# Fused two-layer block on one core: eight expert steps over the undispatched tiles stand behind the dispatched row tiles, with gates, result slots and routing drawn elsewhere

## The reference, cut to what matters

```python
logits = normed @ router_w.T
probs = softmax(logits)
top_v, top_i = top_k(probs, 2)
gates = softmax(top_v)
comb = sum(one_hot(top_i, E) * gates[..., None], axis=1)
for e in range(E):
    out = out + comb[:, e, None] * swiglu(normed, gate_up_w[e], down_w[e])
out = out + swiglu(normed, shared_gate_up_w, shared_down_w)
x = x + tanh(g_ffn[1]) * out
```

## Time and profile before

| what | value |
|---|---|
| median of 3 runs | 319.88 us (319.79 to 321.32) |
| the profiled execution | 319.61 us |
| its span in the trace | 317.8 us |
| TensorE matmul, busy | 268.3 us (84%) |
| VectorE, busy | 236.4 us (74%) |
| ScalarE, busy | 204.4 us (64%) |
| GpSimd, busy | 158.9 us (50%) |
| mean granted clock of TensorE | 0.941 |

### The profile page before, as it was taken

How to read it: one execution, slowest core, us unless ns; L and a number is a source line. 1 busy time by engine, 2 the same in 40 slices (tenths; PEclk the granted TensorE clock), 3 DMA queues, 4 the chain that set the end, 5 groups by cost and what they waited for, 6 DMA issues and landing times.

```text
span 317.8 us, 7526 instructions
## 1 busy us (share of the span) xinstructions
PE 268.3 (84%) x2406; PEld 201.9 (64%) x2406; DVE 236.4 (74%) x711; ACT 204.4 (64%) x469; POOL 158.9 (50%) x206
## 2 busy tenths in 40 slices
PE   7878986997999797999988853878899999999950
PEld 4553442555677464676766732368799999999940
DVE  3586198857977666788999967998576767677796
ACT  2964799796577588976855543535657575756560
POOL 2624297024622546643024777770047878787531
PEclk9999999899999999999999655879999999999995
DMA  7890003001269999970000011113122223111064
GB/s 211 233 383 10 1 2 132 0 3 19 117 188 185 178 181 180 190 105 0 2 1 24 30 45 40 53 49 88 37 71 68 78 67 87 51 32 33 8 226 132
DMA packets 34612, 28.12 MB, mean 88 GB/s; under 512 B 3072, under 2 KB 32389, under 8 KB 33936
## 3 DMA queue, kind: packets, MB, share of 16 engines
q1 hardware_dynamic: 32192, 23.77, 33.8%
q0 software_dynamic: 2240, 3.72, 3.6%
q10 hardware_dynamic: 144, 0.15, 0.2%
HBM read 14.15 MB, written 14.40 MB: 90 GB/s over the span
## 4 chain that ended last, share of the span: by engine, by line
PE 52%; DVE 30%; ACT 8%; issue 6%; DMA 2%; SPq 1%; POOL 1%; DVEq 0%
PE bank L1195 47%; DVE region_k L912 2%; DVE region_x L1152 2%; DVE top L911 2%; DMA wr<-in 2%; PE bank L1492 1%; DVE bn_raw L870 1%; DVE nm L1001 1%; DVE region_k L1003 1%; DVE x L1141 1%; DVE x L1142 1%; ACT x_hat L540 1%; DVE x L902 1%; PE bank L1419 1%; DVE region_k L969 1%
## 5 line engine op out<-in xcount | busy, mean ns | idle before, releaser
L1177 DVE TENSOR_TENSOR region_k<-region_x,region_k 128x768 f16<-128x768 f32 (+1 forms) x33 | 30.6, 926 | 21.6 <-ACT region_k L714 21.6
L1195 PE MATMUL bank<-w_high,region_k 128*128 (+1 forms) x380 | 37.8, 221 | 6.4 <-DVE x L1171 3.3
L1195 PE MATMUL bank<-w_scaled,w_high 128*128 128x256 f16 x252 | 42.5, 273 | 0.1
L846 POOL DMA_INDIRECT expert_rows<-region_k,slot_dest x22 | 27.1, 1232 | 26.5 <-DVE region_k L1164 19.2
L714 ACT ACTIVATE region_k<-region_x 128x768 f16<-128x768 f32 (+1 forms) x33 | 26.8, 813 | 15.8 <-DVE region_x L1152 13.7
L820 POOL DMA_INDIRECT dispatched_rows<-region_t,slot x28 | 28.8, 1028 | 16.1 <-issue 8.3
L1195 PEld LDWEIGHTS bank<-w_high,region_k 128*128 128x128 f16 x380 | 30.9, 99 | 7.7 <-issue 7.3
L1195 PE MATMUL bank<-w_scaled,w_low 128*128 128x256 f16 x126 | 34.3, 273 | 0.0
L1195 PE MATMUL bank<-w_low,region_k 128*128 (+1 forms) x190 | 34.0, 221 | 0.0
L1152 DVE SCALAR_TENSOR_TENSOR region_x<-bank,region_w 128x768 f32<-128x768 f32 (+1 forms) x33 | 30.4, 920 | 3.2 <-ACT region_w L719 2.2
L1195 PE MATMUL bank<-filler 128*128 128x512 f16 x94 | 26.9, 407 | 3.9 <-DVE region_k L912 2.4
(11 more groups left out here) (242 smaller groups left out, 736.1 us busy)
## 6 DMA issues: line engine op xcount, KB each, us to landing
dispatched_rows<-pad_rows SPq DMA_DIRECT2D x8, 1048.0 KB, 18.8
w_scaled<-in SPq DMA_DIRECT2D x5, 1024.0 KB, 8.0
w_scaled<-dispatched_rows SPq DMA_DIRECT2D x21, 131.0 KB, 2.3
region_q<-expert_rows SPq DMA_DIRECT2D x3, 512.0 KB, 5.0
x<-in SPq DMA_DIRECT2D x4, 256.0 KB, 4.4
region_w<-in SPq DMA_DIRECT2D x2, 512.0 KB, 7.0
out<-x SPq DMA_DIRECT2D x3, 256.0 KB, 2.3
w_scaled<-in SPq DMA_DIRECT2D x1, 704.0 KB, 4.1
```

The lines of the kernel that those rows point to most:

```text
L846: pool.indirect_dma_start(ytok, bass.IndirectOffsetOnAxis(dst[:, n, h:h + 1].bitcast(U32), 0), yv[n % 4][:, h * D:(h + 1) * D], None, boun ...
L1177: dve.tensor_tensor(hsplit[:, v, k:2 * k], hid[:, v, 0:k], hsplit[:, v, 0:k], ALU.subtract).then_inc(hidden_low, 1)
L1195: return pe.matmul(o, l, r, start=start, stop=stop)
```

## The change

- **Steps.** DENSE_FIRST goes from 3 to 0: 4 shared, 21 row tiles, 8 dense steps. There are 33 steps as before.
- **Routing.** For G0 and G1 the turn, logits, route, rank and slots get due times of their own, earlier than before. The sends are split into send0 to send3, one tile each, with new due times.
- **Result slots.** `slot_dest(n)` moves from row step n - 2 to row step n, behind the low part.
- **Bookkeeping.** top2_apart goes to the step of row tile 2, gates_of_all to that of tile 6, ScalarE's tanh to that of tile 4.
- **Gates and sums.** G1 goes from VectorE to ScalarE and GpSimd. ScalarE weights G2 inside the two steps 30 and 31, then G1 and G3. GpSimd adds in the order G2, G1, G3. VectorE sums G0 alone. SyncE loads results in the order G2, G0, G1, G3 and stores G2, G0, G1, G3, G4.

```diff
-DENSE_FIRST = 3
+DENSE_FIRST = 0
...
-C_POOL = {"rstd": -4.6, "early_low": -5.3, "low": -0.9, "rstd2": 6.5, "send": 12.5, "send2": 16.1}
+C_POOL = {"rstd": -4.6, "early_low": -5.3, "low": -0.9, "rstd2": 6.5, "send0": 11.3, "send1": 11.32, "send2": 11.34, "send3": 11.36}
...
-C_PE_AT = {("turn", 11): 19.95, ("logits", 11): 20.6, ("turn", 13): 21.2, ("logits", 13): 21.4, ("rank", 11): 21.5,
+C_PE_AT = {("turn", 3): 11.4, ("logits", 3): 12.4, ("rank", 3): 13.4, ("turn", 7): 15.4, ("logits", 7): 16.4, ("rank", 7): 17.4,
...
-C_ACT_AT = {("turn_out", 11): 20.55, ("norm2", 13): 20.7, ("high", 13): 20.9, ("turn_out", 13): 21.6,
+C_ACT_AT = {("turn_out", 3): 11.9, ("turn_out", 7): 15.9, ("turn_out", 11): 20.55, ("norm2", 13): 20.7, ("high", 13): 20.9, ("turn_out", 13): 21.6,
...
-C_DVE_AT = {("affine", 13): 20.8, ("low", 13): 21.0, ("route", 11): 21.4, ("slots", 11): 21.6,
+C_DVE_AT = {("low", 3): 11.25, ("route", 3): 12.8, ("slots", 3): 13.5, ("low", 7): 15.25, ("route", 7): 16.8, ("slots", 7): 17.5,
...
-C_POOL_AT = {("rstd2", 13): 19.4, ("rstd2", 15): 21.5, ("send2", 7): 21.6, ("send", 11): 21.7, ("send2", 11): 21.8, ("send", 13): 21.9}
+C_POOL_AT = {("send0", 3): 13.45, ("send1", 3): 13.6, ("send2", 3): 13.7, ("send3", 3): 13.8, ("send0", 7): 17.6, ("send1", 7): 17.7,
+             ("rstd2", 13): 18.5, ("send2", 7): 18.6, ("send3", 7): 18.7, ("rstd2", 15): 21.3,
+             **{(f"send{k}", t): t + 10.5 + 0.1 * k for t in (11, 13) for k in range(4)}}
...
-            for g in (0, 2, 1, 3):
+            for g in (2, 0, 1, 3):
                 n = slice(*GROUPS[g])
                 eng.dma_start(yk[:, n, :], ytok_v[:, n, :]).then_inc(x_loaded[g], 16)
-            for g, ready, count in ((2, last_added, 2), (0, sum_done, T), (SPARSE, rows_ready, len(STEPS)), (3, last_added, 4),
-                                    (1, sum_done, 2 * T)):
+            for g, ready, count in ((2, last_added, 2), (0, sum_done, T), (1, last_added, 4), (3, last_added, 6),
+                                    (SPARSE, rows_ready, len(STEPS))):
...
+            def gated_rows(g, c):
+
+                act.wait_ge(gates_done, 1)
+                act.wait_ge(x_loaded[g], 32)
+                for t in range(*GROUPS[g]):
+                    last = act.activation(yk[:, t, c * D:(c + 1) * D], yk[:, t, c * D:(c + 1) * D], ACT.Copy,
+                                          scale=gate[:, t, c:c + 1])
+                last.then_inc(last_gated, 1)
...
-                if s == 0:
+                if s == len(STEPS) - 3:
+                    gated_rows(2, 0)
+                elif s == len(STEPS) - 2:
+                    gated_rows(2, 1)
+                if s == STEP_OF[4]:
...
-            for g in (2, 3):
-                act.wait_ge(x_loaded[g], 32)
+            for g in (1, 3):
                 for c in range(2):
-                    for t in range(*GROUPS[g]):
-                        last = act.activation(yk[:, t, c * D:(c + 1) * D], yk[:, t, c * D:(c + 1) * D], ACT.Copy,
-                                              scale=gate[:, t, c:c + 1])
-                    last.then_inc(last_gated, 1)
+                    gated_rows(g, c)
...
+                elif stage[:4] == "send" and g is not None and g < SPARSE and lo + int(stage[4]) < hi:
+                    if stage == "send0":
+                        pool.wait_ge(padded, 16 * (E + 2))
+                        pool.wait_ge(slots_ready, g + 1)
+                        pool.wait_ge(ffn_high, g + 1)
+                        pool.wait_ge(ffn_low, g + 1)
+                    send_rows(lo + int(stage[4]))
...
-            for k, (g, c) in enumerate(((2, 0), (2, 1), (3, 0), (3, 1))):
+            for k, (g, c) in enumerate((g, c) for g in (2, 1, 3) for c in range(2)):
...
-            after_hidden = {0: top2_apart, 1: tiles_placed, 2: windows_packed, 3: gates_of_all}
+            after_hidden = {1: tiles_placed, 2: windows_packed, STEP_OF[2]: top2_apart, STEP_OF[6]: gates_of_all}
...
-                ahead = STEPS[s + 2] if s + 2 < len(STEPS) else ("", 0)
-                if ahead[0] == "rows" and ahead[1] >= 2:
-                    slot_dest(ahead[1])
...
-                if ahead[0] == "rows" and ahead[1] < 2:
-                    slot_dest(ahead[1])
+                if s < len(STEPS) and STEPS[s][0] == "rows":
+                    slot_dest(STEPS[s][1])
                 if s == len(STEPS) - 1:
                     dve.wait_ge(x_loaded[0], 32)
                     sum_rows(range(0, 1))
                 elif s == len(STEPS):
-                    sum_rows(range(1, 4))
-            dve.wait_ge(x_loaded[1], 32)
-            sum_rows(range(4, 8))
+                    sum_rows(range(1, 3))
+            sum_rows(range(3, 4))
```

20 lines of the change are left out of this document (6 added, 14 removed).

## The result

The median of four runs is 337.15 us (335.59 to 339.25), against 320.60 us for the kernel before beside it. The ratio is 1.0515, with a 95% interval of 1.0441 to 1.0589. The direction was forecast, the size was not: the forecast was 331.0 us, its range ended at 336.0, and 337.15 lies beyond it.

The account below looks back on a forecast made before the run. VectorE in the second attention, then GpSimd's one-by-one sends, then TensorE from about 226 us bound it. Terms 3.9 - 1.8 + 8.9 + 1.6 + 0.5 + 0.3 - 2.0 = +11.4 on 319.6 gave 331.0 us, range 321.5 to 336.

Parts of the forecast that it names:

- (a): Dense steps: three go from the front to the back and are paid after the row tiles, +8.9 us.
- (f): Gates inside dense steps 30 and 31: more ScalarE scalings and GpSimd additions there, +0.3 us, bounds 0 and 2.
- (b): Second attention: earlier routing of G0 and G1, stall, hops and clock make G2's slots 7.9 us later.
- Rival 1: Attention: the stall behind GpSimd's two sends is partly absorbed, 325.9 us; chance 0.22.
- Rival 3: Attention: TensorE's clock stays lost through it, bound 5 us, 335.5 us; chance 0.15 together with rival 4.
- (c): Sends behind G2's slots: 12 left, 15.9 us from the slots, ending at 217.7, +3.9 us.
- (d): Last send to the rows: -1.8 us, and +1.6 us for the first row tile at half clock.
- (e): Row steps, result slots at their own step: loads fit by 0.3 us; +0.5 us for 17 tiles, bounds 0 and 5.
- rival 4: Row steps: row loads miss their hop at every step by 0.3 us, 336 us; chance 0.15 together with Rival 3.
- (g): Tail: fewer VectorE sums, -3.5 us, and later stores, +1.5 us; together -2.0 us, bounds -4.4 and 0.
- (1): Sign around G1's normalisation: ScalarE waits 5 to 6 us for GpSimd, VectorE about 4.7 us ahead of its affine.
- Rival 2: Attention: no shift of G2's slots, sends end at 209.8; 318.3 us, or 322.3 with the clock lost; chance 0.13.

Follow-up runs that it names:

- e6: The kernel before with DENSE_FIRST 0 alone, all dense steps behind the row tiles: 326.41 us, ratio 1.0149.
- e1: The changed kernel with the two sends of G0 behind the reciprocal root of G1 instead of ahead of it: 328.28 us, ratio 1.026.
- e2: The changed kernel with the result slots drawn two steps ahead again: 334.45 us, ratio 1.0443.
- e4: The changed kernel with the edits of e1 and e2 together: 327.77 us, ratio 1.0223.
- e11: e4 with the bookkeeping of the gates in steps 0 to 3 again: 328.49 us, ratio 1.0253.
- e12: e11 with G1's routing where the kernel before has it, sends as in e9: 326.18 us, ratio 1.0169.
- e13: The kernel before with the result slots alone at each tile's own step, behind the low part: 324.04 us, ratio 1.0113.
- e7: The changed kernel with 20 filler products on TensorE where it stands idle behind the sends of G0: 336.90 us, ratio 1.0472.
- e8: The kernel before with the new end alone (G1 to ScalarE and GpSimd, G2's weights in the last steps, new load and store order): 325.20 us, ratio 1.0102.
- e9: The kernel before with G0's routing alone early, its 8 sends behind G1's reciprocal root, 6 of G1's sends ahead of G4's: 324.07 us, ratio 1.0113.
- e3: The changed kernel with DENSE_FIRST back at 3 and bookkeeping in steps 0 to 3: 336.86 us over four executions; the two that count took 332.48 and 335.53.

## Why the prediction was right or wrong

**(a) The dense steps.** Right: 8.9 forecast, 8.92 in e6, 9.12 in the changed kernel. The 0.3 forecast in (f) for gates inside steps are not there: e1, e2, e4, e11 and e12 have them and the same 28.47 us as e6, which has not. The 0.2 more stand in profiles with late slots, e13 too (19.76 against 19.55).

**(b) The attention.** The mechanism was right, the size too small: 7.9 forecast, 9.9 measured, and both profiles of the changed kernel agree. The stall was 4.65 in the sum and 4.61 in the trace; the early route and hops 2.28 + 0.5 = 2.8 in the sum and some 3.0 by the profiles (the remainder of 9.9). The mis-sized term is the clock behind the stall: 0.5 in the sum, 2.3 in e7's table. The prediction took its 0.5 from a window in which VectorE is busy at half clock; here a group's hop stands in the way at that clock, and VectorE waits for it. Rival 1 (the stall absorbed) is excluded by e1. Rival 3 (the clock lost through all of the attention, 5 us) did not come about: 2.3. The Trainium skill (TensorE: Matmul & The Clock Gate, "What's actually happening") says that activity releases the throttled clock; by that rule, e7 agrees, with 1.00 where the idle TensorE had 0.50 to 0.52.

**(c) The sends.** Right: 15.9 forecast from the end of G2's slots, 15.9 measured (206.30 to 222.21; the table counts from the cast's start).

**(d) From the last send to the rows.** -1.8 and +1.6 were forecast, together -0.2; measured -1.35. The first row hop starts 3.76 us behind the last send's end (222.21 to 225.97), where the sum had 2.35 + 2.3 = 4.65. That is 0.9 of the 1.15 us; the rest lies in the half-clock hops behind it and was not taken apart.

**(e) Result slots at their own step: the step that failed.** The sum gave 0.5 us. The margin of 0.3 us was right, and that a landing of 2.8 misses it; the rows it rested on already had a landing of 3.7 us. But I took the median landing for nearly all tiles and the bounds 0 to 5 for the rest, with the value at the low end. Late slots measured 3.3 us in the changed kernel (against e2; 2.7 in the medians) and 4.7 in the kernel before (e13; 3.6 by the ratio). That is the price of rival 4, which had been given 0.15 together with rival 3, but not its form: the hops are not late by 0.3 at every step, four of them are late by 0.2 to 1.6. Without late slots the time is inside the range (e2, 334.45). The range ended where either the clock or the loads stand at their bound; both were short at once. A margin smaller than the spread of what it must cover is no cover.

**An edit that was costed at nothing.** The prediction names no price for the bookkeeping that moved from steps 0 to 3 into row steps. It costs 1.3 us there (e11 against e4), since VectorE's low part stands behind it. No gain of that size shows in e11's median.

**(f) and (g) The end.** -2.0 forecast, -1.12 measured, and of these only 0.3 by the new end itself (14.7 against 15.02 in e6). One of GpSimd's additions falls on a low part of VectorE and stretches it from 0.96 to 1.40 us, not by 1.2:

```profile
322.43 1.40 DVE L1184 TENSOR_TENSOR region_k<-region_x,region_k 128x768 f16<-128x768 f32 x1 [0.42 <-ACT region_k L727]
```

The Trainium skill (SBUF — State Buffer, "Who interferes with whom") has the two exclude each other for a whole instruction. The addition ran from 321.74 for 1.27 us, so it overlapped the low part's time by some 0.6 us, and the row is 0.44 longer: the trace agrees with the rule, but the price is the part that overlaps, not a whole addition.

**The front.** 2.6 us of the profiled difference lie where the instructions are the same; the sum had nothing for it. In all 17 profiles the engines' instructions up to G0's statistics stand in the same order, and the front takes 146.38 to 150.66 us, by where the clock falls to half. Both profiles of the changed kernel have 149.4, but e8 and e9, which come from the kernel before, have more, and e3, from the changed one, has 146.38. Whether it belongs to a kernel or to an execution stays open.

**The signs.** (1) came for VectorE (4.61 us) and was 6.31 instead of 5 to 6 for ScalarE. (2) came 4.5 us late, 2.6 of it the front and 2.0 the attention. (3), the last send near 218, came at 222.2 for the same reason, with TensorE idle for 3.65 us and at half clock behind it. (4), row steps at 3.19, was wrong. (5) said 14, measured 14.7. Rival 2, no shift of G2's slots, is excluded by the attention's 9.9 us.

## What to carry to other kernels

An instruction that waits for a late event, put ahead of a cheap one on an in-order queue, stalls everyone behind the cheap one: here two sends ahead of four operations of 1.9 us in all cost 5.65 us, and one number in a table takes it back. When a buffer's release moves later, compare the new margin with the longest landing of the profile, not the median. When an experiment gives back less than its mechanism, look for the same loss at another place of its profile: e7 seemed to price the clock at 1.1 us, for it had a half-clock wait elsewhere. And parts of a change may need each other: the new end costs 3.1 us with five dense steps behind it and saves 0.3 with eight, whose place costs 5 to 7.
